# Lightning attention beside a mixture of experts: combining the four tiles of a head in steps 1, 3, 5 and 7

## Time and profile before

| | us |
|---|---|
| median of three timed runs | 1897.66 |
| span of the profiled execution | 1961.1 |
| TensorE matmul busy in it | 1847.6 (94%) |
| VectorE busy | 1210.9 (62%) |
| ScalarE busy | 998.5 (51%) |
| GpSimd busy | 346.9 (18%) |

### The profile page before, as it was taken

One profiled execution on the slowest core, in us unless ns is written; L12 is line 12 of the kernel. 1 busy time (PEld: TensorE's weight loads), 2 busy tenths in 40 slices (PEclk: granted clock), 3 DMA queues, 4 the chain that ended last, 5 costly groups with the idle time before them and its releaser, 6 DMA issues.

```text
span 1961.1 us, 39254 instructions
## 1 busy us (share of the span) xinstructions
PE 1847.6 (94%) x12603; PEld 1635.2 (83%) x12603; DVE 1210.9 (62%) x2452; ACT 998.5 (51%) x1693; POOL 346.9 (18%) x375
## 2 busy tenths in 40 slices
PE   6999997999999999999999998989998989899998
PEld 6888886878888888888888888978897889788987
DVE  7888885855445455454555556665666566656665
ACT  4334443455565555665556554544454545454542
POOL 2331577720000000000000013030303030303011
PEclk9999997999999999999999999999999999999998
DMA  6665333333443434434334332020202020202014
GB/s 217 219 236 194 105 123 107 122 107 123 129 126 122 128 120 124 136 119 127 123 120 139 122 94 79 4 78 4 73 9 78 4 78 4 78 4 70 12 57 151
DMA packets 175779, 199.38 MB, mean 102 GB/s; under 512 B 19744, under 2 KB 155168, under 8 KB 175648
## 3 DMA queue, kind: packets, MB, share of 16 engines
q1 hardware_dynamic: 150944, 138.87, 22.8%
q0 software_dynamic: 12288, 33.57, 5.4%
q10 hardware_dynamic: 12416, 25.17, 3.4%
HBM read 111.54 MB, written 86.00 MB: 101 GB/s over the span
## 4 chain that ended last, share of the span: by engine, by line
PE 80%; another core or an unknown queue 6%; issue 4%; DVE 4%; ACT 3%; DMA 1%; SPq 0%; DVEq 0%; ACTq 0%
PE bank L1232 6%; PE bank L1340 6%; PE bank L1233 5%; PE bank L1321 5%; PE bank L1234 5%; PE bank L1245 5%; PE bank L1247 5%; PE bank L1246 5%; PE bank L1328 5%; PE bank L1342 5%; PE bank L1281 4%; PE bank L1290 3%; PE bank L1260 3%; PE bank L1310 3%
## 5 line engine op out<-in xcount | busy, mean ns | idle before, releaser
L1245 PE MATMUL bank<-wh,xc 128*128 128x256 f32 x1024 | 304.6, 297 | 12.9 <-issue 12.9
L1247 PE MATMUL bank<-wh,xc 128*128 128x256 f32 x1024 | 290.7, 284 | 0.9 <-issue 0.9
L1246 PE MATMUL bank<-wl,xc 128*128 128x256 f32 x1024 | 290.2, 283 | 0.3 <-issue 0.3
L719 ACT ACTIVATE o<-bank 128x512 f32<-128x512 f32 x128 | 76.6, 599 | 354.3 <-PE bank L1342 244.1
L581 POOL COPY picked<-pos 128x4 uint32 x32 | 11.3, 353 | 1274.1 <-DMA slot_y<-ys 746.3
L1232 PE MATMUL bank<-xh,wh 128*128 (+1 forms) x512 | 226.2, 442 | 9.2 <-DVE state L1047 5.7
L1245 PEld LDWEIGHTS bank<-wh,xc 128*128 128x128 f32 x1024 | 197.1, 193 | 12.9 <-issue 12.9
L1233 PE MATMUL bank<-xl,wh 128*128 (+1 forms) x512 | 207.8, 406 | 0.0
L1234 PE MATMUL bank<-xh,wl 128*128 (+1 forms) x512 | 206.9, 404 | 0.0
L1340 PE MATMUL bank<-sm,kv 128*128 128x128 f32 x1024 | 197.9, 280 | 1.3 <-DVE state L1034 0.8
L1246 PEld LDWEIGHTS bank<-wl,xc 128*128 128x128 f32 x1024 | 197.2, 193 | 1.6 <-issue 1.6
(11 more groups left out here) (176 smaller groups left out, 4071.6 us busy)
## 6 DMA issues: line engine op xcount, KB each, us to landing
slot_x<-zeros ACTq DMA_DIRECT2D x8, 3072.0 KB, 10.0
we<-wexp_in SPq DMA_DIRECT2D x192, 128.0 KB
xs<-slot_x SPq DMA_DIRECT2D x96, 256.0 KB
slot_y<-ys SPq DMA_DIRECT2D x96, 256.0 KB, 2.2
wd<-wdown_in SPq DMA_DIRECT2D x192, 64.0 KB
raw<-wqkv_in SPq DMA_DIRECT2D x17, 384.0 KB
xin<-x_rows SPq DMA_DIRECT2D x8, 512.0 KB, 4.0
xn_rows<-xn SPq DMA_DIRECT2D x8, 512.0 KB, 5.4
```

Of the source, the lines that this page charges most:

```text
L1245: pe.matmul(dst, lh, rh, start=(k == 0), stop=False)
L1246: pe.matmul(dst, lh, rl, start=False, stop=False)
L1247: mm = pe.matmul(dst, ll, rh, start=False, stop=(k == KD - 1))
```

## The change

In heads 8 to 15 `combine` of tiles 0, 1, 2 and 3 now stands ahead of steps 1, 3, 5 and 7. All of steps 1 to 7 of these heads are written out for VectorE; the loop over steps 5 and 6 is gone there. The weights are taken over in step 4 as before. Heads 0 to 7 keep their code, and no other engine's program is edited.

```diff
--- before.py
+++ after.py
@@ -1076,23 +1076,23 @@
                     t0 = (h - GATHER) * CH
                     n0 = (h - GATHER) * 2
                     step(h * NSB, 0, NSB - 1, par, experts, False, beside, (), h + 1, start)
-                    for b in range(1, SB_PER_SEQ) if gather else ():
-
-                        combine(t0 + b - 1, n0 + (b - 1) // 2, (b - 1) % 2)
-                        step(h * NSB + b, b, b - 1, par, experts, b == SB_PER_SEQ - 1)
+                    for b in range(1, NSB) if gather else ():
+
+                        weights_of = (h + 1, 1 - par) if b == SB_PER_SEQ else ()
+                        if b % 2:
+                            combine(t0 + b // 2, n0 + b // 4, b // 2 % 2)
+                        step(h * NSB + b, b, b - 1, par, experts, b % SB_PER_SEQ == SB_PER_SEQ - 1, (), weights_of)
                     if not gather:
                         with dve.Fori(1, SB_PER_SEQ - 1) as b:
                             step(h * NSB + b, b, b - 1, par, experts, False, beside, (), None, start)
                         b = SB_PER_SEQ - 1
                         step(h * NSB + b, b, b - 1, par, experts, True, beside, (), None, start)
-                    b = SB_PER_SEQ
-                    if gather:
-                        combine(t0 + CH - 1, n0 + 1, 1)
-                    step(h * NSB + b, b, b - 1, par, experts, False, beside, (h + 1, 1 - par), None, start)
-                    with dve.Fori(SB_PER_SEQ + 1, NSB - 1) as b:
-                        step(h * NSB + b, b, b - 1, par, experts, False, beside, (), None, start)
-                    b = NSB - 1
-                    step(h * NSB + b, b, b - 1, par, experts, True, beside, (), None, start)
+                        b = SB_PER_SEQ
+                        step(h * NSB + b, b, b - 1, par, experts, False, beside, (h + 1, 1 - par), None, start)
+                        with dve.Fori(SB_PER_SEQ + 1, NSB - 1) as b:
+                            step(h * NSB + b, b, b - 1, par, experts, False, beside, (), None, start)
+                        b = NSB - 1
+                        step(h * NSB + b, b, b - 1, par, experts, True, beside, (), None, start)
                 return run
```

## The result

The changed kernel takes 1905.49 us (median of 20 runs, 1897.37 to 1909.14) against 1898.67 us for the kernel before (20 runs beside them, 1893.75 to 1906.15). The ratio is 1.0029 with a 95% interval of 1.0019 to 1.0039: 0.3% slower, by 4 to 7 us. I had forecast no change.

The account below looks back on a forecast made before the run. The prediction took TensorE to bound the kernel, at 80% of the chain that ended last. Its five terms were each 0, so it forecast no change, 1897 us, with a range of 1887 to 1904 for 8 times in 10.

Parts of the forecast that it names:

- What the gathers disturb: Heads 8 to 15, pauses of TensorE's results during moved gathers: 0 for timed runs, -18 to +8 us if real.
- The weight load: Next head's weights, asked for in step 7 instead of 4, still land 5.4 us before they are wanted: cost 0.
- a rival with a chance of 0.13: TensorE's three jumps back meet the gather and weight load; if their waits double, 7.8 us slower, 1905.5 us; chance 0.13.
- Most of the pauses come with the recording: Heads 8 to 15: TensorE's late-reported results, some 64 us, taken as mostly absent from timed runs, with close to bare steps.
- A combination costs nothing: VectorE's idle time before `qp` covers each combination at old and new places: 0.
- the longer distance: Gather of tiles 2 and 3 gets two steps instead of one; nothing waited before, so the gain is 0.
- L893 has one wait for `raw`: Sign in the trace after: L893 has no wait for `raw`.
- L1140 never waits for a load: Third phase: `res_a` and `res_b` land in time despite the later last store, cost 0; sign: L1140 does not wait for `res_a`.
- The written-out code costs nothing: VectorE in heads 8 to 15: about a seventh more code and no loop, cost 0.
- step 0 of heads 10, 12 and 14: Place to look at, along with L893, if timed runs rise over 1901.5 us.

Follow-up runs that it names:

- r1: The changed kernel, unchanged, run again on a quiet chip (one without pauses): 1905.53 against 1898.65 us, ratio 1.0032.
- b1: The kernel before, unchanged, profiled once more on a quiet chip (one without pauses): 1897.59 us against 1898.00 for its own other runs, ratio 1.000.
- e8: The kernel before with TensorE's program written out for all of heads 2 to 15: 1881.15 us, ratio 0.9896.
- e4: The changed kernel with combinations ahead of steps 1, 2, 3 and 7, so only the fourth is late: 1906.53 us, ratio 1.0040 to the kernel before.
- e1b: The changed kernel with the next head's weights asked for in step 4, only the gather late, quiet chip: ratio 1.0001 to the kernel before.
- e7: The kernel before with only the weight load late (SyncE waits for step 7's gate projection), gather early, quiet chip: ratio 1.0002.
- e1: The changed kernel with the next head's weights asked for in step 4, on a chip with pauses: ratio 1.0072 to the kernel before.
- e2: The changed kernel with combinations ahead of steps 1, 3, 5 and 6, on a chip with pauses: ratio 1.0161 to the kernel before.
- e5: The changed kernel with TensorE's program for heads 8 to 15 written out, without its jump: 1885.52 us, ratio 0.9924 to the kernel before.
- e6: The kernel before with TensorE's program for heads 8 to 15 written out, without its jump: 1883.65 us, ratio 0.9921.
- e3b: The changed kernel's written-out VectorE steps with combinations in their old places, ahead of steps 1, 2, 3, 4, quiet chip: ratio 0.9996 to the kernel before.
- e9: The kernel before with VectorE's program for heads 8 to 15 written out, so VectorE does not jump back and TensorE does: ratio 0.9983.

## Why the prediction was wrong

**The step that failed** is the sum's term "What the gathers disturb", which I set to 0 because I looked only at steps and pauses, together with "The weight load", which I checked for being in time and not for what it runs beside. Both moved to a place where TensorE waits for code, and that place was a rival with a chance of 0.13. Its mechanism was right: three jumps, the gather and the weight load beside them, 7.8 us if the waits doubled, 1905.5 us. The run gave 1905.49. That the two figures agree is luck. By the traces the waits did not double but went from 9.7 to 14.1 us, 4.4 us more; timed, with and without the jump, the loss is 20.0 - 15.0 = 5.0 us, where the two terms had 0. I had judged the rival from waits of 2.0 to 3.6 us. Those were of a chip with pauses, and at two of those three jumps the two fetches of code were apart.

One trace of each kernel would not have shown the size. The spans of r1 and b1 differ by 6.8 us, but the first steps of heads 10, 12 and 14 by 2.5 us only, for b1 lost more to the slow clock. Another 2.5 us lie at the first steps of heads 4 and 6, which the change does not touch.

The Trainium skill, "Runtime: NRT & Kernel Launch", section "Instruction fetch mechanics", says that a taken branch to code outside the current two-page window has to wait for a DMA fetch of it. The runs agree: TensorE waits 1.8 to 5.4 us at its jumps, and in e8, which has no jump in heads 2 to 15, not at all there. The prediction drew from that section that other transfers would make the wait longer. The section does not say so itself; e4, e1b and e7 show it.

**The jump costs more than its wait**, since the clock falls. The windows of the changed kernel run again (r1) at the jump to head 12 (us, PE, PEld, DVE, ACT, POOL busy, PEclk, DMA share, GB/s):

```profile
1518.00:1519.00 1.00, 0.00 (x0) 0.00 (x0) 0.00 (x0) 0.00 (x0) 0.69 (x2) 1.00 0.31 105
1519.00:1520.00 1.00, 0.60 (x3) 0.63 (x4) 0.00 (x0) 0.00 (x0) 0.70 (x2) 0.79 0.47 148
1520.00:1521.00 1.00, 1.00 (x7) 1.00 (x6) 0.00 (x0) 0.00 (x0) 0.71 (x1) 0.50 0.47 139
1521.00:1522.00 1.00, 1.00 (x7) 1.00 (x6) 0.00 (x0) 0.00 (x0) 0.00 (x0) 0.50 0.46 131
1522.00:1523.00 1.00, 1.00 (x6) 1.00 (x6) 0.00 (x0) 0.60 (x1) 0.00 (x0) 0.50 0.03 8
1523.00:1524.00 1.00, 1.00 (x9) 1.00 (x9) 0.00 (x0) 0.00 (x0) 0.00 (x0) 1.00 0.00 0
```

After the idle time the granted clock is 0.50 (1.2 GHz, the lower of its two levels) for some three and a half microseconds. So the step is 17.39 us: 10.84 bare, 4.82 waiting, and 1.7 for the slow clock. In b1 the kernel before has the low clock for about twice as long at the same jump:

```profile
1510.00:1511.00 1.00, 0.00 (x0) 0.00 (x0) 0.61 (x1) 0.00 (x0) 0.00 (x0) 0.72 0.00 0
...
1516.00:1517.00 1.00, 1.00 (x5) 0.90 (x5) 0.00 (x0) 0.42 (x1) 0.00 (x0) 0.50 0.00 0
1517.00:1518.00 1.00, 1.00 (x5) 0.77 (x5) 0.00 (x0) 0.18 (x1) 0.00 (x0) 0.87 0.00 0
```

It pays 3.0 us for it (17.09 = 10.84 + 3.28 + 3.0) after a shorter wait, and that is why the steps of the two kernels differ less than their waits.

**The pauses.** "Most of the pauses come with the recording" was wrong: a chip with pauses takes 1948 us with nothing but timing. The 0 that I drew from it came true for the runs that made the result, but only because they were quiet: with pauses, e1 and e2 are 0.7% and 1.6% slower than the kernel before with their combinations at other places.

**Right, point by point.** A combination costs nothing that can be told at its new places (e5 and e6 are within the error). No combination waited for its gather, before or after, so the longer distance gained nothing. L893 has one wait for `raw`, of 2 us, in head 8, and the kernel before has the same one on a quiet chip. L1140 never waits for a load. The written-out code costs nothing (e3b, 0.9996). And the prediction named the place to look at if the time rose: step 0 of heads 10, 12 and 14.

## What to carry to other kernels

When work moves to a later place, ask not only whether it is in time there but what else needs DMA at that place; a loop's jump back is such a place, and here its wait for code grew with each of the two loads beside it. Writing out the loop of the bounding engine gave 1%, more than any order of the combinations. When a profiled execution is 3% off the timed runs, take another profile before weighing terms of a few us, as its waits may be of another condition of the chip.

## What was not expected of the hardware

- One wait at TensorE's jump is 1.8 to 5.4 us with the same program of TensorE (e9 and e4). The wait goes with what its two 16 KB fetches run beside and whether they come together.
- The clock falls to 0.50 at most of these jumps but not at every one, and what it costs does not grow with the wait. In the nine quiet traces it cost nothing at 5 of the 27 jumps and 1.5 to 3.0 us at the others. After 2.98 us idle at the jump to head 10 in the changed kernel, step 0 took 13.93 us, 0.1 more than 10.84 plus the wait; after 3.28 us in b1 the clock cost 3.0.
- TensorE's reports can come 2 to 3 us late during gathers in all runs of one job, and in none of another job on the same chip: 50 us, 2.6%.
